# An AdaLN transformer block with a perturbed two-expert FFN: the fill written out ahead of the loop, softmax divided two head groups at a time, router logits with tokens on the rows, and fewer unread matmuls

## What is computed

```python
mod = (silu(c) @ wmod).reshape(8, 6, 1, 128)      # sa, ca, ga, sb, cb, gb
ga, gb = sign(g) * max(|g|, 0.25)                  # sign(0) counts as +1
h = layernorm(x) * (1 + ca) + sa
x = x + ga * attention(h)        # 16 heads of 8, ALiBi, causal, softmax, W_o
h = layernorm(x) * (1 + cb) + sb
x = x + gb * ffn(h)
```

## Time and profile before

| | |
|---|---|
| median of 3 runs | 246.72 us (244.29 to 246.96) |
| the profiled execution's own time | 246.49 us |
| its span, first to last instruction | 244.8 us |
| granted TensorE clock, mean | 0.993 |
| busy: PE / PEld / DVE / ACT / POOL | 217.0 / 143.6 / 195.2 / 169.4 / 143.2 us |

### The profile page before, as it was taken

The page is one execution under the profiler, slowest core; times in us unless marked ns, Lnnn a source line. Parts: engine busy times, 40 slices in busy tenths (PEclk is TensorE's granted clock), DMA queues, the critical chain, the costliest instruction groups (busy, mean ns, idle before and its releaser), DMA issues.

```text
span 244.8 us, 5563 instructions
## 1 busy us (share of the span) xinstructions
PE 217.0 (89%) x1848; PEld 143.6 (59%) x1864; DVE 195.2 (80%) x621; ACT 169.4 (69%) x401; POOL 143.2 (58%) x232
## 2 busy tenths in 40 slices
PE   5898888989988989987979879997998999999993
PEld 2454555655655766564656646664554687764783
DVE  2549999999899999999999888884897394764474
ACT  2336767999999988998968967974668552354220
POOL 7652051495887986997585433563859808190710
PEclk9999999999999979999999999999999999999999
DMA  6544673894843722714431500000000001010011
GB/s 198 102 137 143 162 195 98 210 252 130 201 119 98 173 76 83 187 49 122 119 88 60 139 3 5 0 3 3 3 0 1 3 0 44 3 43 0 3 43 44
DMA packets 19155, 20.45 MB, mean 84 GB/s; under 512 B 1367, under 2 KB 17382, under 8 KB 18062
## 3 DMA queue, kind: packets, MB, share of 16 engines
q1 hardware_dynamic: 18438, 19.76, 30.8%
q10 hardware_dynamic: 688, 0.33, 0.5%
HBM read 14.70 MB, written 5.26 MB: 82 GB/s over the span
## 4 chain that ended last, share of the span: by engine, by line
PE 49%; DVE 30%; ACT 11%; issue 8%; DMA 1%; DVEq 0%; ACTq 0%
PE bank L891 12%; PE bank L873 8%; DVE nmax L1165 8%; PE bank L688 4%; DVE msk L1136 4%; ACT msk L560 4%; PE bank L790 3%; DVE nmax L1161 3%; ACT PT L548 3%; DVE cand L1148 2%; PE bank L965 2%; PE bank L856 2%; PE bank L769 2%; PE bank L836 2%; PE bank L747 2%
## 5 line engine op out<-in xcount | busy, mean ns | idle before, releaser
L489 POOL TENSOR_SCALAR_AFFINE_SELECT PT<-PT 128x256 f32<-128x256 f32 (+1 forms) x96 | 45.3, 486 | 38.1 <-ACT PT L548 36.1
L548 ACT ACTIVATE PT<-bank 128x512 f32<-128x512 f32 x96 | 54.8, 608 | 4.2 <-PE bank L764 2.7
L1165 DVE TENSOR_REDUCE nmax<-bank 128x2 f32<-128x512 f32 x64 | 43.3, 681 | 1.9 <-PE bank L747 1.5
L560 ACT ACTIVATE msk<-w2a,cand 128x512 bf16<-128x512 f32 x60 | 43.0, 729 | 0.0
L462 POOL TENSOR_TENSOR ex<-eul,lg 128x32 f32<-128x32 f32 x4 | 21.7, 5436 | 20.2 <-DVE lg L1227 20.2
L560 ACT ACTIVATE msk<-w1a,cand 128x512 bf16<-128x512 f32 x31 | 22.9, 737 | 6.2 <-DVE cand L1148 5.9
L769 PE MATMUL bank<-Qs,Ks 80*128 80x256 bf16 x128 | 24.8, 276 | 0.7 <-ACT PT L548 0.4
L747 PE MATMUL bank<-Ks,Qs 78*128 78x256 bf16 x128 | 24.5, 274 | 0.0
L1136 DVE TENSOR_SCALAR_CACHE_REDUCE msk<-w1a,cand 128x512 bf16<-128x512 f32 x31 | 23.1, 746 | 1.1
L743 PE MATMUL bank<-mask 128*128 128x256 bf16 x64 | 17.8, 279 | 5.5 <-DVE nmax L1165 4.7
L1161 DVE TENSOR_REDUCE nmax<-bank 128x4 f32<-128x512 f32 x32 | 21.6, 675 | 1.1 <-PE bank L740 0.8
(11 more groups left out here) (200 smaller groups left out, 511.4 us busy)
## 6 DMA issues: line engine op xcount, KB each, us to landing
Qs<-parts SPq DMA_DIRECT2D x7, 576.0 KB
Ks<-parts SPq DMA_DIRECT2D x7, 576.0 KB
parts<-part SPq DMA_DIRECT2D x7, 384.0 KB, 2.8
rows_bc<-rows_out SPq DMA_DIRECT2D x8, 192.0 KB, 7.9
x_all<-in_x SPq DMA_DIRECT2D x8, 128.0 KB, 7.0
parts<-part SPq DMA_DIRECT2D x8, 128.0 KB, 2.9
out<-ob SPq DMA_DIRECT2D x3, 256.0 KB, 2.3
w_sb<-in_w SPq DMA_DIRECT2D x2, 256.0 KB, 5.1
```

The lines of the kernel that those rows point to most:

```text
L489: gp.affine_select(out=v, in_=v, compare_op=ALU.is_ge, fill=0.0, base=0, pattern=[[0, v.shape[1]], [1, P]], channel_multiplier=-1).then_in ...
L548: act.activation(PT[:, e % 2, j], psE[u % 2][:, :], ACT.Exp).then_inc(q["exp_done"], 1)
L560: act.activation(msk[:, col], w[:, :], ACT.Sign, bias=cand[:, col:col + 1].bitcast(F32), scale=-(1.0 - 2.0 ** -24), accum_out=acc[:, col:c ...
L1165: ve.tensor_reduce(nmax[:, b % 2, 1, h:h + 2], bank.rearrange("p (h k) -> p h k", h=2), axis=AX.X, op=ALU.max, negate=True).then_inc(q["ma ...
```

## The change

The loop now starts at step 0 on every engine, and the fill is written out ahead of it, each engine with an order of its own. Five things change:

1. **The fill.** SP loads x of batch 0 first, only the two wmod columns that are needed early, then x of batch 1 ahead of W1 and W2; the rest of wmod has its own semaphore. PE starts with 6 unread matmuls before the transpose of c, then 2, 2, 5 and 4 in the fill (19). DVE normalises x of batch 0 before it writes the projection weights. The first candidate is made ahead of `first_split`, and the first two rounds of the search lie between the projections of batches 0 and 1.
2. **The small constants.** The vector columns and two of the modulation rows move from DVE to ACT and into steps 0 and 1, the router constants to step 2. `gate_signs` has two DVE instructions instead of three. `rows_to_dram` is issued behind `write_parts(2)`.
3. **Two groups at once.** psU holds the transposed results of two groups; reciprocal and division run in every second step over 8 heads.
4. **Logits by token rows.** `c_pe_l` issues four products with h2T as weights (128x128) and wrg moving (8 columns), directly into psX. `c_act_l` and `c_pe_t` are gone. For pair 0 it stands in step 36.
5. **No unread matmuls in the loop**: neither the 4 nor the 2 per step in steps 0 to 4.

The core of the diff, with the new orders:

```diff
-            for t in range(T_FIRST, T_END):          # PE
+            turned(0)
+            pe.wait_ge(q["wo_in"], 16)
+            tr(psO[:, 0:P], wo_in[:, :], ident[:, :]).then_inc(q["pe_set"], 1)
+            spare(2)
+            projected(0)
+            spare(5)
+            values(0)
+            pe.wait_ge(q["modrow_in"], 16)
+            mm(psE[1][0:B, 0:512], c_s[:, :], wmod_sb[:, 2 * D:6 * D], start=True, stop=True).then_inc(q["pe_set"], 1)
+            turned(1)
+            total(0)
+            projected(1)
+            spare(4)
+            vectors()
+            total(1)
+            values(1)
+
+            for t in range(T_END):
...
                 if n is not None and t < E_LAG:
                     total(n)
-                    spare(2)
...
                 s_unit(t, 2)
-                if AT_QK < t < E_LAG:
-                    spare(4)
...
+            scaled(0)                                # ACT
+            act.wait_ge(q["w1_in"], 16)
+            act.activation(w1a[:, :], w1_sb[:, :], ACT.Abs).then_inc(q["act_set"], 1)
+            first_parts()
+            sign_count(0, 2, w1a)
+            value_copy(0)
+            act.wait_ge(q["w2a_done"], 1)
+            sign_count(0, 3, w2a)
+            scaled(1)
+            sign_count(1, 2, w1a)
+            high_parts(1)
+            sign_count(1, 3, w2a)
...
+            first_cand()                             # DVE
+            v.wait_ge(q["w2_in"], 16)
+            absolute(w2a[:, :], w2_sb.rearrange("p c d -> p (c d)")).then_inc(q["w2a_done"], 1)
+            first_split()
+            v.wait_ge(q["w2a_done"], 1)
+            v.wait_ge(q["act_set"], ACT_SETS["w1a"])
+            dve_counts(0)
+            ln1(2)
+            decide(0)
+            next_cand(0)
+            dve_counts(1)
+            after_next(0)
+            remainder(1)
+            gate_sizes()
+            decide(1)
+            next_cand(1)
+            dve_counts(2)
+            after_next(1)
+            gate_signs()
...
-                if b is not None:
+                if b is not None and g % 2:
                     v.wait_ge(q["ut_done"], e + 1)
-                    ve.reciprocal(rden[:, :, :], psU[:, 0:S].rearrange("p (i h r) -> p i h r", i=NBLK, h=HG)[:, :, :, HD]
-                                  ).then_inc(q["rd_done"], 1)
+                    pu = psU.rearrange("p (i h r) -> p i h r", i=NBLK, h=2 * HG)
+                    ve.reciprocal(rden[:, :, :], pu[:, :, :, HD]).then_inc(q["rd_done"], 1)
...
             def c_pe_l(p):
                 pe.wait_ge(q["h2T_done"], p + 1)
-                mm((psE[1] if p else psX)[0:NE, :], wrg[:, :], h2T[:, p % 2], start=True, stop=True).then_inc(q["lgT_done"], 1)
-
-            def c_pe_t(p):
-                pe.wait_ge(q["lgT_out"], p + 1)
                 claim_x((q["lg_read"], p + 1))
                 for i in range(4):
-                    last = tr(psX[:, i * NE:(i + 1) * NE], lgT[:, i * P:(i + 1) * P], ident[0:NE, 0:NE])
+                    last = mm(psX[:, i * NE:(i + 1) * NE], h2T[:, p % 2, i * P:(i + 1) * P], wrg[:, :], start=True, stop=True)
                 last.then_inc(q["lg_psum"], 1)
```

More of the change, by code:

```diff
@@ L494, in _ @@
                 b = batch_at(t, AT_N1)
-                if b:
+                if b is not None:
                     normal(b)
                 b = batch_at(t, AT_SPLIT)
-                if b is not None and b >= OWN_SPLIT:
+                if b is not None:
                     lower_parts(b)
@@ L902, in total, with turned, projected, values @@
                 mm(psX[:, 0:4], ones_f[:, :], acc[:, :], start=True, stop=True).then_inc(q["tot_done"], 1)
-            for t in range(T_FIRST, T_END):
+            def turned(b):
+                pe.wait_ge(q["n1_done"], b + 1)
+                if b == 0:
+                    pe.wait_ge(q["dve_set"], SETS["silu"])
+                else:
+                    pe.wait_ge(q["v_out"], b)
+                for i in range(NBLK):
+                    last = tr(psQ[:, i * P:(i + 1) * P], n1[:, b % 2, i, :], ident[:, :])
+                last.then_inc(q["t_done"], 1)
+            def projected(b):
+                pe.wait_ge(q["h1_done"], b + 1)
+                if b == 0:
+                    pe.wait_ge(q["dve_set"], SETS["wk"])
+                for a in range(2):
+                    bank = psS[1][:, 0:S] if a and b == 0 else psQ[:, a * S:(a + 1) * S]
+                    last = mm(bank, wqkT[:, a, :], h1T[:, b % 2], start=True, stop=True)
+                    if a == 0 and b == 0:
+                        last.then_inc(q["q0_done"], 1)
+                last.then_inc(q["qk_done"], 1)
+            def values(b):
+                pe.wait_ge(q["res_done"], b + 1)
+                if b == 0:
+                    pe.wait_ge(q["dve_set"], SETS["wv"])
+                for i in range(NBLK):
+                    last = mm(psQ[:, i * P:(i + 1) * P], h1T[:, b % 2, i * P:(i + 1) * P], wvT[:, :], start=True, stop=True)
+                last.then_inc(q["v_done"], 1)
+            turned(0)
+            pe.wait_ge(q["wo_in"], 16)
+            tr(psO[:, 0:P], wo_in[:, :], ident[:, :]).then_inc(q["pe_set"], 1)
+            spare(2)
+            projected(0)
[10 more added lines that the diff above has]
+            values(1)
+            for t in range(T_END):
                 n = sel_bit(t)
@@ L1312, in perturb_b2, with remainder @@
                 tiers(psX[:, 0:P], psX[:, P:2 * P], b2_bc[:, :], b2p_bc[:, :], b2t[:, :], K_B2, "b2p_done")
-            for t in range(T_FIRST, T_END):
+            def remainder(b):
+                v.wait_ge(q["hi_done"], b + 1)
+                v.wait_ge(q["split_done"], b)
+                pq = psQ.rearrange("p (a t) -> p a t", a=2)
+                ve.tensor_tensor(resid[:, :, :], pq, part8[:, b % 2, 0:4:3, :], op=ALU.subtract).then_inc(q["res_done"], 1)
+            first_cand()
[17 more added lines that the diff above has]
+            gate_signs()
+            for t in range(T_END):
                 n = sel_bit(t)
```

262 lines of the change are left out of this document (106 added, 156 removed).

## The result

The changed kernel took **244.09 us** (median of 20 runs, 241.91 to 246.45) against 246.72 us of the kernel before on the same chip; the ratio is 0.989, with an interval from 0.986 to 0.992. So it is faster, by 1.1% and not by the 3% that was forecast, and 244.09 lies outside the range. The profiled execution took 245.93 us (span 244.2): it is one of the four longest of the 20, 1.8 us over the median, at a mean granted clock of 0.933 where the fastest (241.91 us) had 0.955.

A forecast was written before the change was run, and what follows sets the result against it. DVE was taken to bind the loop with ACT right behind, PE the tail, waits the fill. 4.3 + 0.1 - 1.0 + 2.1 + 1.7 + 0.4 = 7.6 us off 246.49 gave 238.9 us, range 235.3 to 243.3.

The forecast's parts named there:

- The fill: Before step 0: the search starts at the end of the first split; gain 4.3 us, ends 3.0 and 5.5.
- the count: In the fill: search rounds added up from the split at 12.5 us to the decision at about 21.7, 9.2 us.
- The clock: Steps 0 to 4: without unread matmuls PE runs partly at 1.2 GHz; loss 1.0 us, ends 0 and 2.5.
- Two groups at once: Loop: paired reciprocal and division save DVE 0.17 us per step; gain 2.1 us, ends 0 and 3.6.
- The rival's outcome: Loop: ACT binds at once and pairing brings nothing; 241.0 us, chance 0.13.
- Logits: Tail: a pair costs 8.11 us instead of 8.69, three times; gain 1.7 us, ends 1.0 and 2.3.
- The 0.4 us of steps 33 and 36: Pair 0's logits leave step 33 for step 36, an ACT copy gone; gain 0.4 us, ends 0.1 and 0.95.
- the matmuls taken out: Steps 0 to 4: 30 unread matmuls leave PE, little of it on the path; gain 0.1 us after DVE's router constants.
- its own signs of being wrong: Fill and loop: wrong if step 0 started later than 21 us, or the loop's steps were no shorter.
- the clock falls often: Loop: PE stays at 1.2 GHz into the full steps; gain gone at 15 us, 250 us at 22; chance 0.05.

The follow-up runs named there:

- e1: The changed kernel with the 30 unread matmuls of steps 0 to 4 put back: 243.12 us, ratio 0.987.
- e15: The changed kernel with batch 1's remainder on DVE moved behind the decision and candidate of round 1: 243.22 us, ratio 0.989.
- e5: The changed kernel with batch 1's part writes held in SyncE's queue until batch 0's stack has landed: 245.86 us, ratio 0.999.
- e10: The changed kernel with 12 unread matmuls added at the fill's end and the 30 of steps 0 to 4 put back: 239.87 us, ratio 0.974.
- e3: The kernel before with only the pairing added (reciprocal and division of two head groups at once): 247.36 us, ratio 1.001.
- e8: The kernel before with one extra 128x32 copy on DVE in each of 26 steps: 247.84 us, ratio 1.008.
- e4: The kernel before with only the router logits by token rows added: 244.94 us, ratio 0.996.
- e16: The changed kernel with unread matmuls in fill and steps 0 to 4, batch 1's remainder behind round 1's decision and candidate: 240.15 us, ratio 0.974.
- e9: The changed kernel with 12 unread matmuls added at the fill's end alone, steps 0 to 4 staying without: 242.74 us, ratio 0.989.
- e2: The kernel before with only the 30 unread matmuls of steps 0 to 4 taken out: 249.74 us, ratio 1.013.

## Why the prediction was wrong, by its steps

**The fill: right, a little high.** Forecast 4.3 us, decision of step 0 at 21.7. It came at 22.68, 3.3 us early, and at 21.43 in e1, which has the same fill: loads that arrive earlier or later move it by over 1 us from run to run. Two terms of the count were off. The first split ended at 12.99 + 0.42 = 13.41 us, not at 12.5 and not ahead of the 13.16 of before: DVE stood 2.19 us for the probe table, which was there at 11.23 us and not at about 10. (In e1 it was there at 10.01.) From the split to step 0's decision it then took 9.3 us, as the 9.2 that were counted, but 0.8 us of them are DVE held by GpSimd (e15), which the count had left out; against it stand terms that were too high, as two sign counts, which take 1.52 us (17.66 to 19.18 in the kernel before) and not 1.8. The stack landed at 24.8 and not at 22.4, beside batch 1's part writes, which now go out 4.7 us earlier than before (19.73 against 24.39) and so meet it; PE waited 0.47 us for it at step 1, and 1.27 us in e15. Taking the wait away brought nothing (e5).

**The clock: the failed step.** The forecast took 1.0 us, the middle of 0 and 2.5, and saw the spell inside steps 0 to 4. Measured from step 0's decision to step 6's scores it cost 24.26 us (46.94 - 22.68) against 19.99 (45.99 - 26.00): **4.3 us**. With both sets of unread matmuls (e10) the same stretch took 20.34 us (43.76 - 23.42), so 3.9 of the 4.3 us went with the clock, and e10 as a whole is 4.2 us faster than the changed kernel by the medians, 3.7 by the ratios. Three errors are in it. The unread matmuls of the new fill were not laid beside its idle times: the forecast counted PE's work in the steps, but the clock fell at 20.5 us, between the gaps of 1.16 and 1.61 us that the faster fill had opened. The spell did not end with step 4: step 5, the first with full work, ran at 0.50 and took 5.36 us instead of 3.16, 2.2 us by itself; from the decision to step 5 the loss was 2.1 us (18.90 against 16.83), inside the forecast's ends. And the price was taken from a spell in a full step, where 1.1 us was the most. Here DVE has nothing else to do: its waits for PE from step 0 to step 6 went from 0.2 to 3.5 us. The Trainium skill, in "TensorE: Matmul & The Clock Gate" (What's actually happening), has throttled as the default state. The trace agrees: the second stretch of the kernel after ran at 0.51 throughout. By it the forecast had 2.5 us, about what those steps cost; the 2.2 us of step 5 were not in it.

**Two groups at once: wrong.** Forecast 2.1 us, measured 0 in the loop, and within 0.3 us behind it. The lengths were right but for the reciprocal (248 ns, not 210). But they overlap the next instruction. Counted up to its start, the two together took 3.0 us less from step 6 to step 31 in e3, not some 4, and DVE's busy time there fell by only 1.5 us (107.00 to 105.51), as other instructions took more. The rival's outcome is right (nothing), its reason is not shown: DVE pays for what it gets too (e8). In 15 of 25 steps DVE's normalisation is not on the path, and where it is, gain and loss cancel. The view to read was the chain of waits in the loop, not the sum of busy times: DVE's waits for the total, for one, went from 1.2 us (3 times) to 3.2 us (7 times). The low clock is not the reason: at a clock of 1.00 throughout, from step 6 to step 31, they were 1.7 us (4 times) in e4 and 3.2 us (7 times) in e16.

```profile
DVE cond L1142 <- PE bank L902: 1.2, 3, 0.4
```

```profile
DVE cond L1173 <- PE bank L925: 3.2, 7, 0.7
```

(Waits of DVE between step 5 and 140 us, before and after: total us, times, longest.)

**Logits: right, and low.** Forecast 1.7, measured 2.4 us: 0.79 us per pair instead of 8.69 - 8.11 = 0.58, because the logits came at 0.79 and not 0.90 us and the first layer at 3.54 and not 3.63. The 0.4 us of steps 33 and 36 did not come (27.42 us from step 31 to the tail, 27.49 before). Alone in the kernel before, the new logits gave 0.9 us in all (e4), so the sizes hold for the tail and not for the whole time.

**The sum** of the profiled executions, measured: fill -3.3, to step 6 +4.3, steps 6 to 31 +0.9 (116.37 against 115.44; the granted clock was 0.97 and 0.94 there in places, while e10 took 116.13 with one spell and e16 115.34 without), to the tail -0.1, tail -2.4. That is -0.6 us, the difference of the spans. The forecast's -7.6 missed 3.3 us at the clock, 3.0 in the loop, of which 2.1 is the pairing, 1.0 in the fill, 0.3 ahead of the tail and 0.1 at the matmuls taken out; 0.7 us came unforecast in the tail. Of its own signs of being wrong one came: the steps of the loop were no shorter (116.37 against 115.44 us).

The rival "the clock falls often" had the mechanism that decided, a low clock from step 0 on into the full steps. But it was written as the case in which 15 us or more of the full steps run low, at a chance of 0.05. Measured were 6.2 us (41.58 to 47.8), at 2.2 us; this smaller spell, which also starts before step 0, was in no case.

## What to carry to other kernels

An unread matmul is not waste until its absence was priced: lay PE's idle times of the **new** order, fill included, beside each one taken out. If the clock is lost ahead of a latency-bound stretch, unread matmuls put back too late stand in the way before they help (e1), and those in the first gap alone only put the fall off (e9): here both had to be there (e10). And an engine that is busiest on average need not pay for its savings: look in the chain, step by step, in how many of them the instruction stands on it at all.

## What the runs showed of the hardware

The clock also shows in whole runs of one kernel: of e10's six, two at a mean granted clock of 1.00 took 238.87 and 239.50 us, three at 0.989 to 0.993 took 239.07 to 240.72, and that at 0.986 took 242.55. "TensorE: Matmul & The Clock Gate" of the Trainium skill (What's actually happening) gives under 1% of a typical span, but for the ramp. A stage at the low level cost more here: e2 lost 1.3%, and the changed kernel against e10 some 1.5%.

The clock row of the first microseconds cannot be taken as read. It says 1.00, but the six unread matmuls at 1.04 us of the kernel after took 2.74 us, 0.46 each, where four at 16.21 us took 1.03, 0.26 each. The four projection matmuls before (2.07 us at 9.28 us) were slow in the same way: the same four took 1.13 us at 15.24 us in the kernel after.

Two DVE instructions of 0.16 and some 0.4 us took 1.01 and 1.10 us when they met GpSimd's 1.15 us subtraction, and ended 0.02 us and 0.28 us behind it, while a count of DVE took its usual 0.74 us beside GpSimd's cast. The Trainium skill, in "SBUF — State Buffer" (SBUF: two separate sides), has GpSimd and a DVE operation with two SBUF inputs exclude each other for the whole instruction, if GpSimd's reads SBUF. Both slow instructions have two such inputs, and in these two places the trace agrees. It does not everywhere: the same candidate took its usual 0.16 us at 66.95 us, beside 0.84 us that were left of a GpSimd instruction with an SBUF input (L476).

It is not a matter of the fill alone. Of the 60 candidates and successors (`cand`, `nxt`) that DVE makes in the search, 28 took over 0.19 us instead of 0.16 in the kernel after, 6.9 us more in all, and 32 in the kernel before, 6.7 us more. Of the 28, 22 began beside a causal mask of GpSimd and 4 beside its subtraction, and 24 of these 26 ended within 0.04 us of it. How much of that lies on the path was not tested.
